# A float32 transformer block on one core: the output projection's first loads moved into attention's last head, and one small subtraction moved from VectorE to GpSimd

## The chip, the cores and the metric

One core of a Trainium2 chip. The metric is the device time of one execution in microseconds; the profile is of one such execution. TensorE is called PE, VectorE DVE, ScalarE ACT, GpSimd POOL and SyncE SP, as the profile calls them.

## The reference, cut to what matters

X has 2 sequences of 2048 tokens of 256 numbers. Four blocks follow, each added to its input: linear attention, a mixture of 16 experts (2 chosen), softmax attention, a mixture of 64 experts (8 chosen). The change is in the third:

```python
q, k, v: (2, 16 heads, 2048, 64)
scores = einsum('bhqd,bhkd->bhqk', q, k) * scale
attn = softmax(scores, axis=-1)
out = einsum('bhqk,bhkd->bhqd', attn, v)
out = out.transpose(0, 2, 1, 3).reshape(b, s, H * DH) @ w_out.T + residual
```

[...]

## The kernel before, in words

The stages run one after the other, with a barrier of all engines between them (`release`): linear attention, 16 experts, projections of q, k and v, softmax attention (`softmax_attention`), output projection with router (`output_projection`), 64 experts (`expert_pairs`).

**Softmax attention.** There are 32 heads in all (2 sequences x 16), `g` = 0 to 31, in 16 pairs (`pr`, `hh`). A head has 4 blocks of 512 queries (`qb`), a block has 8 slots, a slot `n` (0 to 31 in its head) is 512 queries against 256 keys. In a slot:

- PE makes the scores of slot n+2 (four matmuls of 512 columns, L1863 and L1864), the values of slot n (five, L1879, L1880 and L1882; six for the last slot of a block) and two matmuls of raw scores 13 slots ahead (L1847), from which only a maximum is taken. At the first slot of a block it also adds the block before's sums by a matmul, the fold (L1889).
- ACT makes `ph`, the exponential rounded to fp32r (L1815), and the same unrounded in place (L1818).
- DVE takes the low part `pl` of the exponential of slot n+1 (`low_part`, L1744) and the maximum of raw scores (`maxima`, L1724). Scores of slot n+2 wait for `pl` of slot n, because they use its PSUM.
- POOL multiplies `ph` by the low part of the first value column and adds it up (`first_sums`, L1650 to L1661: one product and one sum in each slot, none in a block's last slot). ACT's `ph` of slot n waits until the sums of slot n-4 are made; the fold waits for the last sum of its block, written to `accr`.

Once per block, in the slots with n % 8 = 2, DVE makes the stabilisers of the next block from 16 maxima (`stabilisers`, L1726 to L1737): `mg` (L1732, f32), `mh` (L1735, the same rounded to fp32r) and `ml` = `mg` - `mh` (L1737), and SP brings `mh` and `ml` as two rows into `q2` (`rows`, L1509 to L1514), for which the first scores of that block wait. In the slots 7, 9, 11 and 13 of a head DVE also cuts the raw queries and keys of the next head (`cut_low`, L1710), and POOL subtracts the cut in slots 8, 10, 12 and 14 (`take_low`, L1630). POOL splits the next head's values in the slots from 16 on (L1607, L1612, L1619), and adds two halves of a block's output in each slot with n % 8 = 5 (`whole`, L1666). The order of every engine's work is written out by hand: each engine has one stream in program order, and semaphores join them.

The excerpt that matters most, DVE's and POOL's:

```python
dve.tensor_reduce(mg[:], every, X, ALU.max).then_inc(s["mg_ready"], 1)
dve.tensor_reduce(mh[:, qb], every, X, ALU.max).then_inc(s["mg_ready"], 1)
dve.wait_ge(s["mg_ready"], 2 * (base * NQB + (qb + 1)))
dve.tensor_tensor(ml[:, qb], mg[:], mh[:, qb].bitcast(F32), ALU.subtract).then_inc(s["nm_ready"], 1)

for n in range(SLOTS):                       # POOL, head()
    first_sums(g, hh, n)
    if n % PER == 5 and g * NQB + n // PER > 0:
        whole(...)
```

**Output projection.** 8 chunks of 512 tokens. SP's queue loads, in this order: the picking matrix `sel_in` (L2009), the attention outputs and reciprocal rows of chunk 0 (`load(0)`, L1982 to L1986), the weights `wo` and `wg` (L2011, L2012), x, the softmax sums `dn` (L2014), chunk 1, x, chunk 2. ACT rounds the picking matrix (L2174) when `sel_in`, `wo` and `wg` are all there. PE waits for that and for the rows of a chunk, and spreads a reciprocal row over 128 partitions (`spread`, L2214), DVE multiplies the outputs by it (`norm`, L2058), 8 times in a chunk, and then PE multiplies with `wo` (`out_tile`, L2221). `spread(1, 0)` comes on PE right behind the first of chunk 0's four `out_tile`s.

Of the kernel before, what the change touches and what calls it, by code (L numbers as in the profile page):

```python
# [26 lines left out]
P = 128  # L27
# [6 lines left out]
QB = 512  # L34
# [106 lines left out]
class Kernel:  # L141
# [4 lines left out]
    def build(self):  # L146
# [14 lines left out]
        with ExitStack() as keep:  # L161
            self.C = keep.enter_context(nc.sbuf_tensor("C", [P, sum(w for _, w in CONST)], F32))
            self.tri = keep.enter_context(nc.sbuf_tensor("tri", [P, P], BF16))
            self.ones_bf = keep.enter_context(nc.sbuf_tensor("ones_bf", [P, P], BF16))
            self.eps = keep.enter_context(nc.sbuf_tensor("eps", [P, 2], F32))
            with ExitStack() as pw:
# [12 lines left out]
                self.raw0 = self.wup[:, 0:2].rearrange("p w n -> p (w n)").bitcast(F32R)  # L179
                self.project()  # L180
                self.release()
                self.softmax_attention()
            with ExitStack() as moe1:
                self.WR = 18
                self.sid = moe1.enter_context(nc.sbuf_tensor("sid", [P, E1 // 2], U32))
                self.sid_up = moe1.enter_context(nc.sbuf_tensor("sid_up", [CAP, E1 // 2], U32))
                self.wgu1 = moe1.enter_context(nc.sbuf_tensor("wgu1", [P, self.WR, DC, 2 * F1], F32))
                self.wd1 = moe1.enter_context(nc.sbuf_tensor("wd1", [F1 // 2, self.WR, 2, D], F32))
                self.output_projection()
                self.expert_pairs()  # L190
            self.release()
# [1217 lines left out]
    def softmax_attention(self):  # L1409
# [16 lines left out]
        with ctx:  # L1426
# [5 lines left out]
            cut = sb("cut", [P, 2, QB], U32)  # L1432
            low = sb("low", [P, 2, QB], F32R)
            vf = sb("vf", [P, 2, KC, DH])
# [23 lines left out]
            names = ("turns raw0 raw1 kq0 kq1 v0 v1 fixed cut_ready low_ready low0 low1 u_full u_max mg_ready nm_ready "  # L1458
                     "row0 row1 row2 row3 s_full p_ready pf_ready pl_ready vh_ready v_split pv_done scaled sums vl0_ready vx_ready fold_done o_added o0_low o1_low "
                     "o_ready o0_out o1_out den recip rden").split()  # L1460
# [26 lines left out]
            def _(sp):  # L1487
# [80 lines left out]
                for pr in range(1, PAIRS - 1):  # L1568
                    for hh in range(2):
# [18 lines left out]
            @block.gpsimd  # L1588
            def _(pool):
# [43 lines left out]
                def first_sums(g, hh, n):  # L1633
# [5 lines left out]
                    for j in range(2):  # L1639
# [21 lines left out]
                        pool.tensor_tensor(to, acc[:], add, ALU.add).then_inc(s["sums"], 1)  # L1661

                def whole(g, qb):

                    pool.wait_ge(s[f"o{qb % 2}_low"], 16 * ((g * NQB + qb) // 2 + 1))
                    pool.tensor_tensor(o_st[:, qb % 2], o_lo[:, qb % 2], o_all[0:DH, qb % 2], ALU.add).then_inc(s["o_added"], 1)  # L1666

                def head(pr, hh, prepare):
                    g, nxt = pr * 2 + hh, pr * 2 + (hh + 1)
                    for n in range(SLOTS):  # L1670
                        first_sums(g, hh, n)
                        if n % PER == 5 and g * NQB + n // PER > 0:
                            whole((g * NQB + n // PER - 1) // NQB, (n // PER - 1) % NQB)
# [29 lines left out]
            def _(dve):  # L1703
# [22 lines left out]
                def stabilisers(base, hh, j):  # L1726
# [71 lines left out]
            def _(act):  # L1798
# [121 lines left out]
    def output_projection(self):  # L1920
# [13 lines left out]
        with ctx:  # L1934
            wo = sb("wo", [P, G, D])
            wg = sb("wg", [P, DC, E1])
            self_in = sb("sel_in", [4 * G, G, P])
            pick = sb("pick", [4 * G, G, P], F32R)
# [4 lines left out]
            oT = sb("oT", [P, OB, G, CH])  # L1943
            rows = sb("rows", [4 * G, OB, CH], F32R)
            xs = sb("xs", [P, 2, TC, D])
# [23 lines left out]
            ps_v = ps("ps_v", [P, CH])  # L1969
            names = ("turns weights den recip low_ready rden pick_ready r_ready norm_ready o0 o1 o2 r0 r1 r2 x0 x1 out_ready added "  # L1970
                     "x0_out x1_out stat mv_ready std_ready own ln_ready xn_ready xn0_out xn1_out t_ready xT_ready l_ready "
# [7 lines left out]
            def _(sp):  # L1979
                def load(c):  # L1980
                    b, at = c * CH // L, slice(c * CH % L, c * CH % L + CH)
                    sp.dma_start(oT[:, c % OB], self.o_dram[b * G:(b + 1) * G, :, at].rearrange("g p l -> p g l"))\  # L1982
                        .then_inc(s[f"o{c % OB}"], 16)
                    for part in range(2):
                        sp.dma_start(rows[part * 2 * G:(part + 1) * 2 * G, c % OB].bitcast(F32),
                                     self.rden[part, b * 2 * G:(b + 1) * 2 * G, at]).then_inc(s[f"r{c % OB}"], 16)  # L1986
# [63 lines left out]
            def _(dve):  # L2050
                link = Chain(dve, s["own"])

                def norm(c, g):
                    if c >= NC:
                        return
                    dve.wait_ge(s[f"o{c % OB}"], 16 * (c // OB + 1))
                    dve.wait_ge(s["r_ready"], c * G + g + 1)
                    dve.tensor_tensor(oT[:, c % OB, g], oT[:, c % OB, g], ps_r[:, g % 2], ALU.mult).then_inc(s["norm_ready"], 1)  # L2058

# [104 lines left out]
            def _(act):  # L2164
# [37 lines left out]
            def _(pe):  # L2202
                pe.wait_ge(s["weights"], 48)
                pe.wait_ge(s["pick_ready"], 1)

                def spread(c, g):
# [3 lines left out]
                    if g == 0:  # L2210
                        pe.wait_ge(s[f"r{c % OB}"], 32 * (c // OB + 1))
                    if c > 0 or g > 1:
                        pe.wait_ge(s["norm_ready"], c * G + g - 1)
                    pe.matmul(ps_r[:, g % 2], pick[:, g], rows[:, c % OB], start=True, stop=True).then_inc(s["r_ready"], 1)  # L2214

                def out_tile(c, t):
# [3 lines left out]
                    for g in range(G):  # L2220
                        m = pe.matmul(ps_o[:, t % 2, 0:D], oT[:, c % OB, g, t * P:(t + 1) * P], wo[:, g],  # L2221
                                      start=g == 0, stop=g == G - 1)
# [283 lines left out]
```

## Time and profile before

| what | value |
|---|---|
| median of 3 runs | 4191.82 us (4189.85 to 4196.26) |
| the profiled execution's own time | 4191.36 us |
| its span, first to last instruction | 4189.6 us |
| mean granted TensorE clock | 0.952 |
| PE, DVE, ACT, POOL busy in the span | 90%, 81%, 63%, 73% |
| softmax attention | about 893 to 3707 us |
| output projection | from 3707 us |

A row of the timeline has the start in us from the span's start, the duration, the engine, the line, the operation with what it writes and reads, and in brackets how long the engine sat idle before it and what ended that. PE's durations overlap, since its matmuls are pipelined: one matmul's price is the time from its start to the next one's.

### The profile page before, as it was taken

The page shows a single profiled execution, that of the slowest core. Times are in us where ns is not written, and L with a number is a line of the kernel's source. Part 1 is how long each engine was busy: PE and PEld are TensorE (multiplying, and loading weights), DVE is VectorE, ACT ScalarE, POOL GpSimd, SP SyncE. Part 2 cuts the span into 40 slices and gives each one's busy share as a digit, 9 for nine tenths or more (in the row PEclk, how much of TensorE's full clock was granted, in tenths as well). Part 3 has the DMA queues.
Part 4 walks back from the last instruction along what each step waited for, and adds up shares of the span by engine and source line. Part 5 has one row for each costly group of instructions (what it writes and reads, how often), then busy time and mean ns, then how long its engine had stood idle before and what let it go on. Part 6 is the DMA issues. An engine that isn't in the chain of part 4 may idle for free. (4 is left out here: it accounts for less than half of the span.)

```text
span 4189.6 us, 55316 instructions
## 1 busy us (share of the span) xinstructions
PE 3758.9 (90%) x17018; PEld 2903.6 (69%) x17018; DVE 3392.4 (81%) x4389; ACT 2623.1 (63%) x3395; POOL 3042.9 (73%) x2832
## 2 busy tenths in 40 slices
PE   7949977869999999999999999999999999979563
PEld 4635545548888888888888888888888888857321
DVE  6845548869999999999999999999999999946511
ACT  6723333337777777777777777777777777733221
POOL 2456765758888888888888888888888888820155
PEclk9969998979999999999999999999999999989676
DMA  7123437852224332242322423224232242046295
GB/s 271 47 65 60 67 78 244 274 160 63 61 58 89 65 65 60 57 92 62 66 59 59 93 60 67 60 57 91 62 66 59 63 88 61 20 160 221 73 248 111
DMA packets 332634, 396.27 MB, mean 95 GB/s; under 512 B 142541, under 2 KB 251922, under 8 KB 319284
## 3 DMA queue, kind: packets, MB, share of 16 engines
q1 hardware_dynamic: 307702, 362.22, 33.9%
q0 software_dynamic: 24640, 30.52, 4.2%
q8 instruction: 140, 2.29, 0.2%
q14 instruction: 152, 1.24, 0.1%
HBM read 232.47 MB, written 117.79 MB: 84 GB/s over the span
## 5 line engine op out<-in xcount | busy, mean ns | idle before, releaser
L1815 ACT ACTIVATE at_ph<-at_ps_s 128x1024 fp32r<-128x1024 f32 x1024 | 1052.7, 1028 | 637.0 <-PE at_ps_s L1864 621.3
L1724 DVE TENSOR_REDUCE at_mx<-at_ps_u 128x2 f32<-128x1024 f32 x1016 | 1239.8, 1220 | 157.5 <-PE at_ps_u L1847 122.1
L1744 DVE TENSOR_TENSOR at_pl<-at_ps_s,at_ph 128x1024 fp32r<-128x1024 f32 x1024 | 1245.8, 1217 | 18.5 <-ACT at_ps_s L1818 17.4
L1818 ACT ACTIVATE at_ps_s<-at_ps_s 128x1024 f32<-128x1024 f32 x1024 | 1032.2, 1008 | 32.6
L1653 POOL TENSOR_TENSOR at_part<-at_ph,at_vl 128x512 f32<-128x512 f32 x768 | 799.0, 1040 | 114.2 <-ACT at_ph L1815 90.2
L1661 POOL TENSOR_TENSOR at_acc<-at_acc,at_part 128x512 f32<-128x512 f32 x640 | 833.5, 1302 | 50.1
L1879 PE MATMUL at_ps_v<-at_ph,at_va 128*128 128x512 f32 x2048 | 812.2, 397 | 1.1 <-DVE at_pl L1744 1.1
L1880 PE MATMUL at_ps_v<-at_pl,at_va 128*128 128x512 f32 x2048 | 812.9, 397 | 0.0
L1882 PE MATMUL at_ps_v<-at_ph,at_vx 128*128 128x512 f32 x1152 | 456.2, 396 | 0.0
L1880 PEld LDWEIGHTS at_ps_v<-at_pl,at_va 128*128 128x128 f32 x2048 | 387.4, 189 | 90.4
L1863 PE MATMUL at_ps_s<-q,k 128*128 128x512 f32 x1024 | 410.9, 401 | 21.6 <-DVE at_pl L1744 19.5
L1863 PE MATMUL at_ps_s<-at_q,at_k 128*128 128x512 f32 x1024 | 411.0, 401 | 20.5 <-DVE at_pl L1744 20.2
L1879 PEld LDWEIGHTS at_ps_v<-at_ph,at_va 128*128 128x128 f32 x2048 | 388.0, 189 | 46.8 <-DVE at_pl L1744 1.7
L1864 PE MATMUL at_ps_s<-at_q,k 66*128 66x512 f32 x1024 | 407.2, 398 | 0.0
L1864 PE MATMUL at_ps_s<-at_q,at_k 66*128 66x512 f32 x1024 | 406.9, 397 | 0.0
L1847 PE MATMUL at_ps_u<-k,q 128*128 128x512 f32 x1008 | 327.3, 406 | 36.6 <-DMA at_q<-at_low 31.3
L1847 PE MATMUL at_ps_u<-at_k,at_q 128*128 128x512 f32 x1024 | 328.7, 402 | 3.8 <-DVE at_mx L1724 3.8
L1847 PEld LDWEIGHTS at_ps_u<-k,q 128*128 128x128 f32 x1008 | 275.0, 311 | 70.2 <-issue 31.7
L1847 PEld LDWEIGHTS at_ps_u<-at_k,at_q 128*128 128x128 f32 x1024 | 279.6, 310 | 34.9 <-DVE at_mx L1724 13.6
L1863 PEld LDWEIGHTS at_ps_s<-q,k 128*128 128x128 f32 x1024 | 193.8, 189 | 89.6 <-DVE at_pl L1744 44.3
L1863 PEld LDWEIGHTS at_ps_s<-at_q,at_k 128*128 128x128 f32 x1024 | 193.4, 189 | 90.0 <-DVE at_pl L1744 47.5
L1882 PEld LDWEIGHTS at_ps_v<-at_ph,at_vx 128*128 128x128 f32 x1152 | 216.2, 188 | 52.6
(285 smaller groups left out, 5446.3 us busy)
## 6 DMA issues: line engine op xcount, KB each, us to landing
wgu<-Wgu_in SPq DMA_DIRECT2D x64, 384.0 KB, 5.1
qT<-pj_rot SPq DMA_DIRECT2D x32, 512.0 KB, 5.2
vT<-pj_vo SPq DMA_DIRECT2D x16, 1024.0 KB, 5.7
kT<-pj_rot SPq DMA_DIRECT2D x32, 512.0 KB, 3.2
k<-kT SPq DMA_DIRECT2D x32, 512.0 KB, 11.6
q<-qT SPq DMA_DIRECT2D x32, 512.0 KB, 9.5
at_q<-at_low SPq DMA_DIRECT2D x128, 128.0 KB, 2.3
at_vf<-vT SPq DMA_DIRECT2D x32, 512.0 KB, 8.7
```

The lines of the kernel that those rows point to most:

```text
L1653: pool.tensor_tensor(add, p, low0, ALU.mult).then_inc(s["scaled"], 1)
L1661: pool.tensor_tensor(to, acc[:], add, ALU.add).then_inc(s["sums"], 1)
L1724: dve.tensor_reduce(mx[:, qb % 2, 2 * i:2 * i + 2], maxima_at(base, j)[:, 0:2], X, ALU.max).then_inc(s["u_max"], 1)
L1744: dve.tensor_tensor(pl[:, n % NP], ps_s[:, n % 2], ph[:, n % NP].bitcast(F32), ALU.subtract)\
L1815: act.activation(ph[:, n % NP], ps_s[:, n % 2], ACT.Exp, scale=DH ** -0.5)\
L1818: act.activation(ps_s[:, n % 2], ps_s[:, n % 2], ACT.Exp, scale=DH ** -0.5)\
L1847: m = pe.matmul(maxima_at(base, j)[:, w], tile, k1[hh][:, kb * QB:(kb + 1) * QB], start=True, stop=True)
L1863: pe.matmul(out, k1[hh][:, ks], q1[hh][:, qs], start=True, stop=False)
L1864: m = pe.matmul(out, k2[hh][0:MROW + 2, ks], q2[hh][0:MROW + 2, qs], start=False, stop=True)
L1879: pe.matmul(out, va[:, hh, c], ph[:, n % NP, keys], start=c == 0, stop=False)
L1880: m = pe.matmul(out, va[:, hh, c], pl[:, n % NP, keys], start=False, stop=False)
L1882: m = pe.matmul(out, vx[:, hh, own_product(c)], ph[:, n % NP, keys], start=False, stop=False)
```

## The change

`ml` is computed by POOL. Its new function `low_stabilisers(block_)` waits for DVE's `mg` and `mh` and stands, in each slot with n % 8 = 2, between `first_sums` and whatever POOL does next; DVE's own wait and subtraction are gone.

```diff
@@ gpsimd
+                def low_stabilisers(block_):
+                    pool.wait_ge(s["mg_ready"], 2 * (block_ + 1))
+                    pool.tensor_tensor(ml[:, block_ % NQB], mg[:], mh[:, block_ % NQB].bitcast(F32), ALU.subtract)\
+                        .then_inc(s["nm_ready"], 1)
@@ head(), gpsimd
                         first_sums(g, hh, n)
+                        if n % PER == 2 and g * NQB + n // PER + 1 < HEADS * NQB:
+                            low_stabilisers(g * NQB + n // PER + 1)
                         if n % PER == 5 and g * NQB + n // PER > 0:
@@ before the heads, gpsimd
+                low_stabilisers(0)
@@ stabilisers(), vector
-                    dve.wait_ge(s["mg_ready"], 2 * (base * NQB + (qb + 1)))
-                    dve.tensor_tensor(ml[:, qb], mg[:], mh[:, qb].bitcast(F32), ALU.subtract).then_inc(s["nm_ready"], 1)
```

The loads of the projection's chunk 0 and of the picking matrix are issued by SP ahead of attention's last head, into buffers of their own (the matrix goes through `raw[0]`, which is free by then), and ACT rounds the matrix at the end of attention. To make room, `low` moves onto a weight buffer that is free in attention.

```diff
@@ build()
+                self.oT0 = early("oT0", [P, H // 2, QB], F32)
+                self.rows0 = early("rows0", [2 * H, QB], F32R)
+                self.pick = early("pick", [2 * H, H // 2, P], F32R)
                 self.softmax_attention()
@@ softmax_attention()
-            low = sb("low", [P, 2, QB], F32R)
+            low = self.wup[:, 2].rearrange("p (i n) -> p i n", i=2).bitcast(F32R)
@@ sync, softmax_attention()
                 head(PAIRS - 1, 0, False, False)
+                sp.wait_ge(s["rden"], 32)
+                sp.dma_start(self.oT0[:], self.o_dram[0:H // 2, :, 0:QB].rearrange("g p l -> p g l")).then_inc(s["next_in"], 16)
+                for part in range(2):
+                    sp.dma_start(self.rows0[part * H:(part + 1) * H].bitcast(F32), self.rden[part, 0:H, 0:QB]).then_inc(s["next_in"], 16)
+                sp.dma_start(raw[0][0:2 * H, 0:H // 2 * P].bitcast(F32), self.ins["sel"]).then_inc(s["pick_in"], 16)
                 head(PAIRS - 1, 1, False, True)
...
-                sp.wait_ge(s["rden"], 32)
+                sp.wait_ge(s["next_in"], 48)
@@ scalar, softmax_attention(), at the end
                 output(HEADS - 1, NQB - 1)
+                act.wait_ge(s["pick_in"], 16)
+                act.activation(self.pick[:], raw[0][0:2 * H, 0:H // 2 * P].bitcast(F32).rearrange("k (g m) -> k g m", g=H // 2),
+                               ACT.Copy).then_inc(s["pick_out"], 1)
@@ sync, output_projection()
-                sp.dma_start(self_in[:], ins["sel"].rearrange("k (g m) -> k g m", g=G)).then_inc(s["weights"], 16)
-                load(0)
@@ scalar, output_projection()
-                act.wait_ge(s["weights"], 48)
-                act.activation(pick[:], self_in[:], ACT.Copy).then_inc(s["pick_ready"], 1)
@@ tensor, output_projection()
-                pe.wait_ge(s["weights"], 48)
-                pe.wait_ge(s["pick_ready"], 1)
...
                 for g in range(G):
                     spread(0, g)
+                pe.wait_ge(s["weights"], 32)
                 for c in range(NC + 2):
```

In the projection `oT` and `rows` are now three tensors each instead of one tensor with three parts, the first of them being `oT0` and `rows0`, and the waits of chunk 0 on their loads fall away.

## Rows read from the trace of the kernel before

**Rows 1.** Windows: busy time of each engine, clock, DMA, in attention and at the projection's start

```profile
core 0: us, PE busy (x) PEld busy (x) DVE busy (x) ACT busy (x) POOL busy (x), PEclk, DMA share, GB/s
915.00:3697.00 2782.00, 2734.51 (x11479) 2255.54 (x11479) 2605.89 (x2543) 2145.99 (x2173) 2376.36 (x2255) 1.00 0.31 65
...
3710.00:3725.00 15.00, 2.92 (x5) 1.34 (x5) 2.37 (x4) 2.34 (x2) 0.00 (x0) 0.50 1.07 366
```

**Rows 2.** Groups by line, 915 to 3697 us: DVE's subtraction and cut, POOL's smallest subtraction

```profile
L1737 DVE TENSOR_TENSOR at_ml<-at_mg,at_mh 128x4 fp32r<-128x4 f32 x127 | 88.1, 694 | 4.4
L1710 DVE TENSOR_SCALAR at_cut<-at_raw 128x512 uint32<-128x512 uint32 x64 | 46.6, 729 | 0.0
...
L1619 POOL TENSOR_TENSOR at_vl<-at_vf,at_va 128x16 f32<-128x16 f32 x31 | 7.6, 246 | 0.0
```

**Rows 3.** Timeline of DVE in head 12 and the next: mh, ml, cut

```profile
1970.42 0.16 DVE L1735 TENSOR_REDUCE at_mh<-at_mx 128x4 fp32r<-128x16 f32 x1
1970.61 1.06 DVE L1737 TENSOR_TENSOR at_ml<-at_mg,at_mh 128x4 fp32r<-128x4 f32 x1
...
1988.03 1.47 DVE L1710 TENSOR_SCALAR at_cut<-at_raw 128x512 uint32<-128x512 uint32 x1
...
1993.02 0.16 DVE L1735 TENSOR_REDUCE at_mh<-at_mx 128x4 fp32r<-128x16 f32 x1
1993.21 0.16 DVE L1737 TENSOR_TENSOR at_ml<-at_mg,at_mh 128x4 fp32r<-128x4 f32 x1
...
2014.41 0.48 DVE L1737 TENSOR_TENSOR at_ml<-at_mg,at_mh 128x4 fp32r<-128x4 f32 x1
...
2080.09 0.16 DVE L1735 TENSOR_REDUCE at_mh<-at_mx 128x4 fp32r<-128x16 f32 x1
```

**Rows 4.** Timeline of PE in head 12: the stalls and the two folds

```profile
1971.90 0.40 PE L1882 MATMUL at_ps_v<-at_ph,at_vx 128*128 128x512 f32 x1
1972.86 0.50 PE L1863 MATMUL at_ps_s<-q,k 128*128 128x512 f32 x1 [0.56 <-DVE at_pl L1744]
1973.20 0.39 PE L1864 MATMUL at_ps_s<-at_q,k 66*128 66x512 f32 x1
...
1990.69 0.86 PE L1847 MATMUL at_ps_u<-k,q 128*128 128x512 f32 x2 [0.28 <-DVE at_mx L1724]
...
2006.80 0.40 PE L1889 MATMUL at_ps_v<-at_accr,at_first 128*128 128x512 f32 x1
...
2028.15 0.39 PE L1889 MATMUL at_ps_v<-at_accr,at_first 128*128 128x512 f32 x1
...
2038.00 0.50 PE L1863 MATMUL at_ps_s<-q,k 128*128 128x512 f32 x1 [0.55 <-DVE at_pl L1744]
```

**Rows 5.** Timeline of POOL in head 12

```profile
1970.36 1.29 POOL L1661 TENSOR_TENSOR at_acc<-at_acc,at_part 128x512 f32<-128x512 f32 x1
...
1987.93 1.30 POOL L1661 TENSOR_TENSOR at_acc<-at_acc,at_part 128x512 f32<-128x512 f32 x1
1989.58 1.28 POOL L1630 TENSOR_TENSOR at_low<-at_raw,at_cut 128x512 fp32r<-128x512 f32 x1 [0.36 <-DVE at_cut L1710]
...
2002.16 1.29 POOL L1661 TENSOR_TENSOR at_accr<-at_acc,at_part 128x512 fp32r<-128x512 f32 x1
...
2022.97 1.29 POOL L1661 TENSOR_TENSOR at_accr<-at_acc,at_part 128x512 fp32r<-128x512 f32 x1
```

**Rows 6.** Timeline, from attention's end to the first output tile

```profile
3707.26 0.34 SPq L2009 DMA_DIRECT2D op_sel_in<-sel_in  x1
...
3720.25 1.05 ACT L2174 ACTIVATE op_pick<-op_sel_in 32x1024 fp32r<-32x1024 f32 x1 [19.86 <-DMA op_wg<-router_in]
3721.41 1.19 PE L2214 MATMUL op_ps_r<-op_rows,op_pick 32*128 32x512 f32 x2 [21.65 <-ACT op_pick L2174]
...
3728.53 5.24 PE L2221 MATMUL op_ps_o<-op_wo,op_oT 128*128 128x256 f32 x16 [0.85 <-DVE op_oT L2058]
```

**Rows 7.** DMA issues, 3697 to 3900 us: KB each, median us to landing

```profile
op_oT<-o_dram SPq DMA_DIRECT2D x8, 2048.0 KB, 9.3
...
op_wo<-w_outT_in SPq DMA_DIRECT2D x1, 1024.0 KB, 9.9
op_rows<-rden SPq DMA_DIRECT2D x16, 32.0 KB, 8.2
```

More of the change, by code:

```diff
@@ L165, in build @@
             self.eps = keep.enter_context(nc.sbuf_tensor("eps", [P, 2], F32))
+            moe1 = keep.enter_context(ExitStack())
             with ExitStack() as pw:
@@ L181, in build @@
                 self.release()
+                early = lambda name, shape, dt: moe1.enter_context(nc.sbuf_tensor(name, shape, dt))
+                self.oT0 = early("oT0", [P, H // 2, QB], F32)
+                self.rows0 = early("rows0", [2 * H, QB], F32R)
+                self.pick = early("pick", [2 * H, H // 2, P], F32R)
                 self.softmax_attention()
[L183 to L190, printed above, removed]
+            self.WR = 18
+            self.sid = moe1.enter_context(nc.sbuf_tensor("sid", [P, E1 // 2], U32))
+            self.sid_up = moe1.enter_context(nc.sbuf_tensor("sid_up", [CAP, E1 // 2], U32))
+            self.wgu1 = moe1.enter_context(nc.sbuf_tensor("wgu1", [P, self.WR, DC, 2 * F1], F32))
+            self.wd1 = moe1.enter_context(nc.sbuf_tensor("wd1", [F1 // 2, self.WR, 2, D], F32))
+            self.output_projection()
+            self.expert_pairs()
             self.release()
@@ L1458, in softmax_attention @@
             names = ("turns raw0 raw1 kq0 kq1 v0 v1 fixed cut_ready low_ready low0 low1 u_full u_max mg_ready nm_ready "
-                     "row0 row1 row2 row3 s_full p_ready pf_ready pl_ready vh_ready v_split pv_done scaled sums vl0_ready vx_ready fold_done o_added o0_low o1_low "
+                     "row0 row1 row2 row3 s_full p_ready pf_ready pl_ready vh_ready v_split pv_done scaled sums vl0_ready vx_ready fold_done o_added o0_low o1_low next_in pick_in pick_out "
                      "o_ready o0_out o1_out den recip rden").split()
@@ L1936, in output_projection @@
             wg = sb("wg", [P, DC, E1])
-            self_in = sb("sel_in", [4 * G, G, P])
-            pick = sb("pick", [4 * G, G, P], F32R)
+            pick = self.pick
             dn = sb("dn", [P, H * L // P])
@@ L1942, in output_projection @@
             rl = sb("rl", [P, H * L // P], F32R)
-            oT = sb("oT", [P, OB, G, CH])
-            rows = sb("rows", [4 * G, OB, CH], F32R)
+            oT = [self.oT0] + [sb(f"oT{i}", [P, G, CH]) for i in range(1, OB)]
+            rows = [self.rows0] + [sb(f"rows{i}", [4 * G, CH], F32R) for i in range(1, OB)]
             xs = sb("xs", [P, 2, TC, D])
@@ L1969, in output_projection @@
             ps_v = ps("ps_v", [P, CH])
-            names = ("turns weights den recip low_ready rden pick_ready r_ready norm_ready o0 o1 o2 r0 r1 r2 x0 x1 out_ready added "
+            names = ("turns weights den recip low_ready rden r_ready norm_ready o0 o1 o2 r0 r1 r2 x0 x1 out_ready added "
                      "x0_out x1_out stat mv_ready std_ready own ln_ready xn_ready xn0_out xn1_out t_ready xT_ready l_ready "
@@ L1981, in load @@
                     b, at = c * CH // L, slice(c * CH % L, c * CH % L + CH)
-                    sp.dma_start(oT[:, c % OB], self.o_dram[b * G:(b + 1) * G, :, at].rearrange("g p l -> p g l"))\
+                    sp.dma_start(oT[c % OB][:], self.o_dram[b * G:(b + 1) * G, :, at].rearrange("g p l -> p g l"))\
                         .then_inc(s[f"o{c % OB}"], 16)
                     for part in range(2):
-                        sp.dma_start(rows[part * 2 * G:(part + 1) * 2 * G, c % OB].bitcast(F32),
+                        sp.dma_start(rows[c % OB][part * 2 * G:(part + 1) * 2 * G].bitcast(F32),
                                      self.rden[part, b * 2 * G:(b + 1) * 2 * G, at]).then_inc(s[f"r{c % OB}"], 16)
@@ L2055, in norm @@
                         return
-                    dve.wait_ge(s[f"o{c % OB}"], 16 * (c // OB + 1))
+                    if c > 0:
+                        dve.wait_ge(s[f"o{c % OB}"], 16 * (c // OB + (c % OB > 0)))
                     dve.wait_ge(s["r_ready"], c * G + g + 1)
-                    dve.tensor_tensor(oT[:, c % OB, g], oT[:, c % OB, g], ps_r[:, g % 2], ALU.mult).then_inc(s["norm_ready"], 1)
+                    dve.tensor_tensor(oT[c % OB][:, g], oT[c % OB][:, g], ps_r[:, g % 2], ALU.mult).then_inc(s["norm_ready"], 1)
                 def add(c, t):
@@ L2210, in spread @@
                     if g == 0:
-                        pe.wait_ge(s[f"r{c % OB}"], 32 * (c // OB + 1))
+                        if c > 0:
+                            pe.wait_ge(s[f"r{c % OB}"], 32 * (c // OB + (c % OB > 0)))
                     if c > 0 or g > 1:
                         pe.wait_ge(s["norm_ready"], c * G + g - 1)
-                    pe.matmul(ps_r[:, g % 2], pick[:, g], rows[:, c % OB], start=True, stop=True).then_inc(s["r_ready"], 1)
+                    pe.matmul(ps_r[:, g % 2], pick[:, g], rows[c % OB][:], start=True, stop=True).then_inc(s["r_ready"], 1)
                 def out_tile(c, t):
@@ L2220, in out_tile @@
                     for g in range(G):
-                        m = pe.matmul(ps_o[:, t % 2, 0:D], oT[:, c % OB, g, t * P:(t + 1) * P], wo[:, g],
+                        m = pe.matmul(ps_o[:, t % 2, 0:D], oT[c % OB][:, g, t * P:(t + 1) * P], wo[:, g],
                                       start=g == 0, stop=g == G - 1)
```

## The prediction, before the change was run

> **What bounds the kernel now.** First the windows by stage: from 915 to 3697 us, two thirds of the span, PE is busy 2734.51 of 2782.00 us at full granted clock, POOL 2376.36, DVE 2605.89 [rows 1]. So attention is PE's, and a gain there has to be a stall of PE that the change removes. The pattern repeats with each head; one period, from `mh` at 1993.02 to the same `mh` of the next head at 2080.09, is 87.07 us [rows 3].
>
> Second the groups by line: `ml`, four numbers per partition, takes DVE 694 ns on average, 88.1 us in all, and the cut 729 ns [rows 2]. The timeline says why these are not short: in one block `ml` takes 0.16 us, in others 0.48 and 1.06 [rows 3]. The one of 1970.61 ends at 1971.67, when POOL's sum of 1970.36 ends at 1971.65 [rows 5]. A DVE instruction that reads two SBUF tiles waits out the GpSimd instruction that is running. The cut of 1988.03 behaves alike: 1.47 us, until 1989.50, with POOL's sum of 1987.93 ending at 1989.23 [rows 3, 5].
>
> Third PE's timeline, where that is paid. PE normally starts a matmul 0.23 us after the last. Here 1971.90 is followed by 1972.86, then 1973.20: 0.73 and 0.11 us lost, 0.84, waiting for `pl`, which stood behind the long `ml`. The stall at 2038.00 (0.55 us idle against 0.56) is its twin in the last block, 0.82. Both vanish without `ml`. The block with `ml` of 0.48 should lose about 0.26 (the 0.84 less the 0.58 by which `ml` is shorter). The fourth loss, about 0.9 around 1990.69, waits for a maximum that stood behind the long cut [rows 3, 4]; there `ml` took 0.16 only and is not the cause. Together about 2.8 us of a head's 87.07.
>
> Fourth the projection. Its first load is issued at 3707.26, PE's first matmul starts at 3721.41 and the first output tile at 3728.53 [rows 6]: 21.27 us in which DMA is the work (share 1.07, 366 GB/s) at half clock [rows 1].
>
> **The projection's part.** Call 3707.26 T0; barrier and SP's order before it stay. The picking matrix, chunk 0 and ACT's rounding (1.05 us [rows 6]) leave the path. PE can spread at about T0 instead of T0+14.15, and the eight spreads and norms take the 7.12 us from 3721.41 to 3728.53: T0+7.1. The weights (1088 KB) are now first in the queue. By the rate of rows 1 they take 3.0 us and some start; from above, `wo` landed after 9.9 us with 2 MB ahead of it [rows 7], so T0+5 to T0+10.4; I take T0+7, hidden behind the norms. The first tile costs 5.24 us as before [rows 6], the clock being at the same half. So 14.2 us are gained up to T0+12.3. Next late is chunk 1: its spread is right behind the first tile, and ahead of its rows 1024+64+512+128+2048 KB, 3.87 MB, go through at 366 GB/s, 10.6 us, plus about 3.7 of start and landing (an estimate; the landing alone is up to 8.2 [rows 7]): T0+14.3. PE waits 2 us. Sum: -12 us, between -9 and -14. Later chunks keep their order and their work, only earlier.
>
> The moved loads are issued around 3610 us, ahead of the last head: 2048 KB land in 9.3 us [rows 7] while DMA is a third busy [rows 1], and the first thing behind them on SP, the low rows of the last head's predecessor, is due only when that head has run two slots. I cost them and ACT's copy at nothing. If that cover is gone, one late row is some 5 us once. The same for moving `low`, and for splitting `oT` and `rows`: other addresses, same work.
>
> **Attention's part, DVE's side.** Removed: 128 waits and subtractions, `mh` is now followed by `pl` at once. That takes 0.84+0.82+0.26 us of PE's stalls away: 85.15 us a head if nothing else is late. At once 31 heads x 1.9 = 60 us.
>
> **Attention's part, GpSimd's side.** Added: 128 subtractions of 128x4. The nearest row is the 128x16 one, 246 ns [rows 2]; I take 0.25. From below, 0.16 as on DVE [rows 3]; from above, 1.30 as the big sums [rows 5], should such an instruction's price lie in its start.
>
> But the wait matters more. In the second block POOL has finished its slot at 1989.23 (1987.93+1.30) and goes on with `take_low` at 1989.58, while `mh` is ready at 1993.18 (1993.02+0.16) [rows 3, 5]. POOL will stand 3.9 us with `take_low` and everything after it queued behind. In the first block it stands 4.3 us too, but has idle time to make that good. From 1989.58 on it has none: it runs without a pause (its timeline has no idle entry) up to the last sum of the third block, which ends at 2024.26: 34.68 us. The folds wait for these sums. Today they have 3.35 us to spare in one block (2002.16+1.29 against 2006.80) and 3.89 in the next (2024.26 against 2028.15) [rows 4, 5]. POOL comes later by 1993.18+0.07+0.25-1989.58 = 3.9 us, and by 4.2 after the second small subtraction, while PE comes earlier. So the folds become late, and the pace is set by a loop through POOL:
>
> - fold at 2028.15 to `mh` ready in the next head, 2080.25: 52.10 today, less the stalls 0.82 and 0.84 in it: 50.4. The cut before this `mh` will meet a product of 1.04 instead of a sum of 1.30; I take 0.2 off: 50.2.
> - `mh` to the last sum of the third block: 0.1 + 0.25 + 34.68 + 0.25 = 35.3.
> - sum to fold: 0.1.
>
> 85.6 us against 87.07: 1.47 x 31 heads = 46 us, of which the loop takes back only 0.45 a head from the 85.15 above. The last head prepares none and adds nothing that I count. The row of `ml` comes to SP later, by the 0.3 us of the subtraction, or by POOL's lag in the third block; it is needed four slots (10 us) on and its transfer is small: hidden.
>
> **Sum against the profiled execution's 4191.36 us:** -12 -46 = 4133, median of the runs 0.5 us above that; I say 4134.
>
> A rule of the Trainium skill speaks against this half. "Perfetto Trace Analysis", section "Optimizing Scalar/DVE Operations", says that GpSimd and VectorE share an SBUF port, so that moving work between the two may not help. The trace shows the shared waiting (0.16 against 1.06 us). By the rule attention would stay, and the sum would be that of the third case below.
>
> **The rivals.** 0.2%, 8.4 us, is about what can be told from no change.
>
> 1. *GpSimd's wait paces attention at about 85.6 us a head* (85.1 to 86.3): 4110 to 4155, point 4134. For: the folds' small spare time and POOL without a pause. Chance 0.52.
> 2. *The cut falls free.* The cut's start and POOL's product before it are within 0.3 us in my walk; if POOL is a little later, the cut costs 0.42 instead of 1.47, `mh` comes 1.05 earlier, the loop is 84.6 and PE's own pace 85.15-0.88 = 84.3. Some 2.5 to 2.8 x 31 = 78 to 87 us: 4092 to 4101. Against: more often GpSimd is running than not (2376 of 2782 us). Chance 0.2.
> 3. *The port's wait comes back at the cuts.* The change would then not do what it says: four cuts a head, 0.729 us on average today, up to 1.47. With POOL shifted by 4 us, three more long ones are 3 us, in the slots where DVE has no slack, and eat up what `ml` gave. Only the projection's 12 remain: 4179, from 4165 to 4190. Against: two of the four come where `take_low` now starts later. Chance 0.18.
> 4. *Slower.* The stretch of GpSimd between `mh` and the last sum of the third block decides from 87.07-50.4-0.1 = 36.6 us; above 37.0 it also eats the projection's 12 us. With a small subtraction at 1.30 us instead of 0.25 it is 34.68+2.6+0.1 = 37.4, the loop 87.9, +0.85 x 31 = +26 -12: 4206. For: GpSimd is given work just where it is fullest. Against: 128x16 costs 246 ns, 31 times. Chance 0.1.
>
> **How the numbers follow.** The forecast is case 1. The range 4088 to 4178 holds cases 1 and 2 and half of case 3, 0.8. Faster by over 0.2% (under 4183): cases 1, 2 and two thirds of 3, 0.83. Within 0.2%: the rest of 3 and some of 4, 0.10. Slower: 0.07.
>
> **What would show it.** In the timeline after: no stall of PE behind `pl` in the first and last block of a head; POOL idle some 4 us before its new subtraction in the first two blocks, none in the third; PE waiting for `accr` before the fold in the second or third block, 0.2 to 1 us; the `mh` to `mh` period about 85.6. The first output tile 7 us after the projection's first load instead of 21.27, and a short wait before `spread(1, 0)`. I am wrong if the small subtraction takes near 1 us, if the cuts' mean moves much from 729 ns, if ACT rather than the fold waits for POOL, or if the first tile waits for weights past T0+10.

## The result, and the profile after

**Slower.** The changed kernel takes 4275.83 us, median of 4 runs (4267.39 to 4284.77), beside 4191.28 us for the kernel before in the same series (4 runs). The ratio is 1.020, with a 95% interval from 1.018 to 1.022: clearly slower, by about 2%. The profiled execution spans 4265.6 us, 76 more than before.

| | before | after |
|---|---|---|
| median of the runs, us | 4191.28 | 4275.83 |
| span of the profile, us | 4189.6 | 4265.6 |
| mean granted clock | 0.952 | 0.943 |
| SP issues the projection's first load at | 3707.26 | 3798.56 |
| from there to the first expert's memset | 247.06 | 233.48 |
| from the memset to the end | 235.3 | 233.6 |
| mean head (from one slot 0's exponential to the next, heads 1 to 30) | 87.10 | 90.29 |

The projection gained 13.6 us and the experts 1.7. Attention lost 91.3, counted up to the projection's first load. First the projection, where the timeline after answers to [rows 6]:

```profile
3798.56 0.42 SPq L2025 DMA_DIRECT2D op_wo<-w_outT_in  x1
...
3798.61 1.19 PE L2225 MATMUL op_ps_r<-rows,pick 32*128 32x512 f32 x2 [7.51 <-PEq L1430]
...
3805.55 6.73 PE L2232 MATMUL op_ps_o<-op_wo,oT 128*128 128x256 f32 x16 [0.87 <-DVE oT L2073]
...
3812.92 0.50 PE L2225 MATMUL op_ps_r<-op_rows,pick 32*128 32x512 f32 x1 [0.65 <-DMA op_rows<-rden]
```

PE spreads at once, and the first tile starts 6.99 us after the first load instead of 21.27. Now attention; first two groups by line from 915 to 3785 us:

```profile
L1727 DVE TENSOR_SCALAR at_cut<-at_raw 128x512 uint32<-128x512 uint32 x64 | 41.5, 649 | 0.0
L1674 POOL TENSOR_TENSOR at_ml<-at_mg,at_mh 128x4 fp32r<-128x4 f32 x127 | 25.5, 201 | 266.0 <-DVE at_mh L1752 266.0
```

The moved subtraction is short, 201 ns where `ml` took 694 on DVE, and the cut of `raw` takes 649 ns instead of 729 [rows 2]. But POOL stands 266 us in front of it. The windows, in the form of [rows 1], show a PE that is busy for less of the time, and a clock that is not full:

```profile
core 0: us, PE busy (x) PEld busy (x) DVE busy (x) ACT busy (x) POOL busy (x), PEclk, DMA share, GB/s
2005.00:2012.00 7.00, 3.36 (x15) 2.57 (x14) 4.75 (x4) 3.04 (x3) 4.97 (x6) 1.00 0.63 127
2013.00:2016.00 3.00, 3.00 (x8) 2.31 (x7) 1.39 (x2) 1.99 (x2) 2.32 (x2) 0.50 0.19 44
915.00:3785.00 2870.00, 2762.78 (x11469) 2292.48 (x11468) 2524.43 (x2414) 2142.47 (x2169) 2384.87 (x2377) 0.98 0.30 64
```

In 915 to 3785 us PE is idle 107 us of 2870, before 47 of 2782. What it waits for is in the waits of that stretch (engine, line, what it waited for: us in total, times, longest):

```profile
POOL at_ml L1674 <- DVE at_mh L1752: 266.0, 96, 6.2
...
PE at_ps_s L1880 <- DMA at_q<-at_ml: 97.7, 31, 3.9
ACT at_ph L1829 <- POOL at_accr L1670: 62.7, 53, 1.5
...
PE at_ps_v L1906 <- POOL at_accr L1670: 5.2, 28, 0.2
```

PE waits for the DMA that carries a row of `ml` into `q`: in each of heads 1 to 30 for 2.5 to 3.9 us at the first scores of the second block, and now and then for a moment elsewhere. PE's waits before have no such line. The 97.7 us are more than attention lost; the timeline of PE after shows one case:

```profile
2007.70 0.40 PE L1899 MATMUL at_ps_v<-at_ph,at_vx 128*128 128x512 f32 x1
2011.74 0.48 PE L1880 MATMUL at_ps_s<-q,k 128*128 128x512 f32 x1 [3.64 <-DMA at_q<-at_ml]
...
2013.09 0.63 PE L1897 MATMUL at_ps_v<-at_pl,at_va 128*128 128x512 f32 x1
...
2014.37 0.63 PE L1896 MATMUL at_ps_v<-at_ph,at_va 128*128 128x512 f32 x1
2014.80 0.63 PE L1897 MATMUL at_ps_v<-at_pl,at_va 128*128 128x512 f32 x1
2015.22 0.63 PE L1899 MATMUL at_ps_v<-at_ph,at_vx 128*128 128x512 f32 x1
```

PE stands 3.64 us. Soon behind the stall the matmuls start 0.43 us apart instead of 0.23: the window 2013 to 2016 has a granted clock of 0.50, the lower of the two levels (1.2 GHz), where the stretch before the stall had 1.00. This does not follow every stall. Of heads 1 to 30, 16 have a stretch of some 3 us at the lower clock, 7 have one of nearly 7 us, and 7 (heads 1, 2, 9 and 26 to 29, with stalls of 2.9 to 3.4 us) have none. The trace thus gives the price by itself: less its own stall, a head takes 85.8 us without the fall, 86.8 with the short one and 88.2 with the long one. On average that is another 1.1 us a head; by the matmuls' spacing it is 1.4.

**Why is the row late?** SP issues it no later in the head than before. Head 12 of the kernel before begins (its first exponential) at 1957.37, the same head after at 1988.05. SP's timeline of the kernel before, rows that were not shown above (SPq is SP's queue; the second column is how long SP issues):

```profile
1953.68 0.47 SPq L1526 DMA_DIRECT2D o_dram<-at_o_st  x1
...
1955.06 0.51 SPq L1489 DMA_DIRECT2D at_raw<-qT  x1
...
1956.97 4.79 SPq L1496 DMA_DIRECT2D at_k<-kT  x1
...
1972.35 0.59 SPq L1514 DMA_DIRECT2D at_q<-at_ml  x1
```

and the same instructions after:

```profile
1989.30 0.47 SPq L1530 DMA_DIRECT2D o_dram<-at_o_st  x1
...
1990.69 0.51 SPq L1493 DMA_DIRECT2D at_raw<-qT  x1
...
1992.59 4.81 SPq L1500 DMA_DIRECT2D at_k<-kT  x1
...
2002.23 0.59 SPq L1518 DMA_DIRECT2D at_q<-at_ml  x1
```

From the head's start the row of `ml` is issued at +14.98 us before and at +14.18 after. The store of the head's third output block moved from -3.69 to +1.25: 4.9 us later. SP issues in order, and behind that store stand the 3.5 MB of loads for later heads: `raw` and `v` (1.5 MB) for the head after next, `q` and `k` (2 MB) for the next. They moved along, and the small rows are now issued while these are still in flight. The row took this long from issue to landing (all 128 rows, of four blocks in each head; first before, then after):

```profile
DMA to landing us min/median/max: 1.9/2.0/4.6
```

```profile
DMA to landing us min/median/max: 1.9/2.0/9.7
```

The long ones are those of the second block: 3.5 us on average before, 9.0 after (heads 1 to 30), where the other blocks' rows keep 2.0 to 2.2. In head 12 the row is issued at 2002.23, PE would take it at 2007.93 (0.23 us after its last matmul), 5.7 us later, and it lands after 9.4 us, at 2011.60. In windows of the trace after, the DMA share is about 1.0 to 1.2 from 1992 to 2007 us, 0.82 from 2007 to 2010 and 0.02 from 2010 to 2012: the row lands when the loads are through.

And why is the store late? It waits for `whole` of slot 29, a sum of POOL. The timelines before and after, rows of POOL and, for `mh` of slot 26 (the last block's), of DVE:

```profile
1948.51 0.16 DVE L1735 TENSOR_REDUCE at_mh<-at_mx 128x4 fp32r<-128x16 f32 x1
...
1952.29 1.29 POOL L1666 TENSOR_TENSOR at_o_st<-at_o_lo,at_o_all 64x512 f32<-64x512 f32 x1
```

```profile
1980.05 0.16 DVE L1752 TENSOR_REDUCE at_mh<-at_mx 128x4 fp32r<-128x16 f32 x1
...
1980.29 0.20 POOL L1674 TENSOR_TENSOR at_ml<-at_mg,at_mh 128x4 fp32r<-128x4 f32 x1 [0.50 <-DVE at_mh L1752]
...
1987.91 1.29 POOL L1680 TENSOR_TENSOR at_o_st<-at_o_lo,at_o_all 64x512 f32<-64x512 f32 x1
...
2001.35 0.20 POOL L1674 TENSOR_TENSOR at_ml<-at_mg,at_mh 128x4 fp32r<-128x4 f32 x1 [3.46 <-DVE at_mh L1752]
...
2027.82 0.20 POOL L1674 TENSOR_TENSOR at_ml<-at_mg,at_mh 128x4 fp32r<-128x4 f32 x1 [4.23 <-DVE at_mh L1752]
```

Before, POOL had gone past slot 26 by the time `mh` was ready: `whole` starts 3.62 us after it (1952.29 less 1948.67). Now POOL's slot 26 cannot begin its subtraction before `mh`, and three slots of sums of 2.56 us stand between it and `whole`, which starts 7.70 us after `mh` (1987.91 less 1980.21).

So the theory to test is a chain through three in-order queues: POOL waits for `mh`, `whole` of slot 29 ends late, SP's store and the 3.5 MB behind it go out late, the row of the second block lands late, PE stalls, and the clock falls behind the stall. Rivals: the long stay of POOL itself paces PE (the loop through POOL, which the prediction's first case rests on, mis-sized); or the fallen clock comes from the new mix of work and not from the stall; or the projection's moved loads are to blame.

### The profile page after: what moved, and what is told of

It reads as the page before. It is cut to its first block and busy times, and to the rows that moved or that the text cites. A ratio compares the mean times of both kernels' runs of the same rounds, so it can differ in the third digit from the quotient of the medians.

```text
span 4265.6 us, 55308 instructions
## 1 busy us (share of the span) xinstructions
PE 3787.4 (89%) x17018; PEld 2942.5 (69%) x17018; DVE 3313.5 (78%) x4261; ACT 2622.2 (61%) x3395; POOL 3056.2 (72%) x2960
## 5 line engine op out<-in xcount | busy, mean ns | idle before, releaser
L1896 PE MATMUL at_ps_v<-at_ph,at_va 128*128 128x512 f32 x2048 | 822.0, 401 | 1.0 <-DVE at_pl L1758 1.0
L1897 PE MATMUL at_ps_v<-at_pl,at_va 128*128 128x512 f32 x2048 | 822.7, 402 | 0.0
L1897 PEld LDWEIGHTS at_ps_v<-at_pl,at_va 128*128 128x128 f32 x2048 | 393.5, 192 | 91.3
```

The costliest lines, as they stand in the source:

```text
L1896: pe.matmul(out, va[:, hh, c], ph[:, n % NP, keys], start=c == 0, stop=False)
L1897: m = pe.matmul(out, va[:, hh, c], pl[:, n % NP, keys], start=False, stop=False)
```

## The experiments

Times are medians, or the one run where there is one; the kernel before stood at 4185.4 to 4191.3 in the series. "Head" is the mean distance of the starts of heads 1 to 31, 87.10 us for the kernel before.

### One half alone: `prefetch_only` and `subtract_only`

`prefetch_only` keeps the projection's part and gives the subtraction back to DVE. `subtract_only` keeps attention's part.

```diff
 # prefetch_only
                     dve.tensor_reduce(mh[:, qb], every, X, ALU.max).then_inc(s["mg_ready"], 1)
+                    dve.wait_ge(s["mg_ready"], 2 * (base * NQB + (qb + 1)))
+                    dve.tensor_tensor(ml[:, qb], mg[:], mh[:, qb].bitcast(F32), ALU.subtract).then_inc(s["nm_ready"], 1)
...
-                        if n % PER == 2 and g * NQB + n // PER + 1 < HEADS * NQB:
-                            low_stabilisers(g * NQB + n // PER + 1)
```

> The change's projection part alone; the subtraction stays on VectorE. All theories: attention stays at 87.1 us a head, the first output tile starts 7 us after the projection's first load instead of 21.3, and the total falls by 13 to 14 us, to about 4178 us. If moving tiles to other addresses or the moved loads had slowed attention, heads would be longer than 87.1 us here.

Measured: 4177.24 us (7 runs) against 4191.03, ratio 0.997 (0.9959 to 0.9982); head 87.06. The first tile starts 6.96 us after SP's first load.

```diff
 # subtract_only
-                sp.dma_start(self.oT0[:], self.o_dram[0:H // 2, :, 0:QB].rearrange("g p l -> p g l")).then_inc(s["next_in"], 16)
...
+                sp.dma_start(self_in[:], ins["sel"].rearrange("k (g m) -> k g m", g=G)).then_inc(s["weights"], 16)
```

> The change's attention part alone. Theory L (late loads: GpSimd's wait in slot 10 makes the half sum 'whole' of slot 29 late, so SyncE issues 3.5 MB of loads late, and the stabiliser rows queue behind them): heads of 90.3 us, a stall of PE of 3.7 us in slot 6 of each head that ends with the DMA of ml, total 4191 + 98 = about 4289 us. If the slow down came from the early loads, the moved tile 'low' or the splitting of oT, this kernel stays below 4191 us.

Measured: 4279.31 us in one run, some 10 us under what was expected; head 90.29, clock 0.942. Its wait for the row:

```profile
PE at_ps_s L1868 <- DMA at_q<-at_ml: 100.7, 32, 4.6
```

The projection's part is a gain of about 14 us, and is cleared. The whole loss is in the subtraction's move.

### Is the DVE gain real: `no_low`

The kernel before, with no subtraction at all: POOL clears `ml` once, and the rows are released by `mh`. It leaves out the low part of the stabilisers.

```diff
-                    dve.tensor_reduce(mh[:, qb], every, X, ALU.max).then_inc(s["mg_ready"], 1)
-                    dve.wait_ge(s["mg_ready"], 2 * (base * NQB + (qb + 1)))
-                    dve.tensor_tensor(ml[:, qb], mg[:], mh[:, qb].bitcast(F32), ALU.subtract).then_inc(s["nm_ready"], 1)
+                    dve.tensor_reduce(mh[:, qb], every, X, ALU.max).then_inc(s["nm_ready"], 1)
```

> No low part of the stabilisers is computed at all: a row of zeros stands in its place, and the rows are released by mh. It prices VectorE's side alone. If the prediction's count of stalls is right: heads of 85.15 us, total 4191 - 60 = 4131 us, with cuts still at 0.7 us on average. If the port's wait comes back at the cuts: heads of 86.5 us or more, 4175 us or more.

Measured: 4128.38 us, head 85.17, with the old projection. The prediction's count of the stalls behind `ml` gave 85.15. The one stall left in a head, 0.6 us, is the one behind the long cut, which stays at 740 ns:

```profile
L1714 DVE TENSOR_SCALAR at_cut<-at_raw 128x512 uint32<-128x512 uint32 x64 | 47.4, 740 | 0.0
```

### The late store alone: `whole_late`

The kernel before, with `whole` one slot later in the last block. No subtraction moves and POOL waits for no `mh`.

```diff
-                        if n % PER == 5 and g * NQB + n // PER > 0:
+                        if n % PER == (6 if n // PER == 3 else 5) and g * NQB + n // PER > 0:
```

> The kernel before, in which only the half sum 'whole' of a head's third block is made one slot later (slot 30 instead of 29), so that SyncE's store, and the 3.5 MB of loads behind it, come 3.5 us later. The stabilisers are as before. Theory L: some 2 us of that are spare, the rest shows as a stall of PE before the first scores of the next head's second block that ends with the DMA of the ml row; with the clock's fall 1.5 to 2.6 us a head, total 4235 to 4270 us. Theory P (only the folds or ACT waiting for GpSimd's sums cost anything) and theory N (the row is late because ml is computed late): within 10 us of 4191 us.

Measured: 4224.96 us, head 88.34, clock 0.952 as before. The row lands after up to 7.4 us, and PE waits for it in 30 heads, which it never did before:

```profile
PE at_ps_s L1863 <- DMA at_q<-at_ml: 28.8, 30, 1.7
```

One line of POOL's order, without any of the change, makes the kernel 34 us slower by the same wait. So the late store alone is enough for a stall of this kind, without any wait of POOL for `mh`; whether POOL's waiting costs something besides, this run does not tell, but the next ones do. It came out under what was expected: `whole` ended at -0.36 us from the head's start (before -3.71, after +1.13), so it is a smaller dose, and behind stalls of 1.2 us on average the clock fell in one head of heads 1 to 30 only, the one with the longest (1.8 us; granted clock 0.50 from 3051 to 3054 us).

### The chain cut on SP: `loads_first` and `store_behind`

Both are the changed kernel, with POOL's order as it is. `loads_first` issues `raw` and `v` (1.5 MB) of the head after next ahead of the late store, and the other 2 MB stay behind it; `store_behind` issues that store behind all 3.5 MB.

```diff
 # loads_first
-                def head(pr, hh, first, last):
+                def head(pr, hh, first, last, next_loads=None):
...
                             rows(*after, 0)
+                        if qb == NQB - 1 and next_loads is not None:
+                            ahead(*next_loads)
                         if block_ > 0:
                             store_o((block_ - 1) // (2 * NQB), (block_ - 1) // NQB % 2, (block_ - 1) % NQB)
...
-                    head(0, hh, True, False)
-                    ahead(0, hh)
+                    head(0, hh, True, False, (0, hh))
```

```diff
 # store_behind
                         load_qk(*after)
+                    if (2 * pr + hh) > 0:
+                        store_o((2 * pr + hh - 1) // 2, (2 * pr + hh - 1) % 2, NQB - 2)
...
-                        if block_ > 0:
+                        if block_ > 0 and (qb < NQB - 1 or last):
```

> The changed kernel, in which SyncE issues the 1.5 MB of raw and value loads ahead of the head's last store instead of behind it, so that only 2 MB stand behind the late half sum. GpSimd's wait is as in the changed kernel. Theory L: the stall of PE in slot 6 (3.7 us) and the fall of the clock behind it vanish, heads of 85.5 to 86.3 us (the loop through the folds of the prediction is then what is left), total 4130 to 4155 us. If GpSimd's lateness costs through anything else (folds, ACT, ml made late), heads stay near 90.3 us and the total near 4270 us.

> The changed kernel, in which the head's last store (of the half sum that is late) is issued behind the 3.5 MB of loads, so that none of them waits for GpSimd. Theory L: as the run loads_first or slightly faster, total 4125 to 4155 us, and PE never waits for the DMA of ml. A theory in which it is the amount of traffic and not its place behind the half sum: no better than the changed kernel.

Measured: `loads_first` 4124.82 us (4 runs), ratio 0.984 (0.982 to 0.986), head 85.34, clock 0.952, the slowest landing 3.7 us. `store_behind` 4120.97 us, head 85.33, slowest landing 3.4 us. Both are some 5 us faster than the ranges on record. The waits for `mh` and for POOL's sums in `loads_first`:

```profile
POOL at_ml L1674 <- DVE at_mh L1752: 218.0, 96, 4.9
...
ACT at_ph L1829 <- POOL at_accr L1670: 63.4, 54, 1.5
```

`loads_first` is the run that decides. POOL stands 218 us for `mh` here too and ends `whole` as late as in the changed kernel (+1.13 us), yet attention takes 85.34 us a head. POOL's waiting costs PE almost nothing by itself. With the stall the falls of the clock in heads 1 to 30 are gone as well, while the work is the same: they belong to the stall and not to the new mix.

### The chain cut on POOL: `slot3` and `slot4`

The changed kernel, with the subtraction one or two slots later in each block.

```diff
-                        if n % PER == 2 and g * NQB + n // PER + 1 < HEADS * NQB:
+                        if n % PER == 4 and g * NQB + n // PER + 1 < HEADS * NQB:    # slot3: 3
```

> The changed kernel with the subtraction on GpSimd one slot later in its program (slots with n % 8 = 3 instead of 2), SyncE's order as in the changed kernel. In the kernel before, the sums of slot 11 ended at the moment at which mh of that block was ready, so the 3.9 us wait there falls to under 0.5 us while the subtraction itself stays on GpSimd. Theory L: half sum of slot 29 on time, no stall in slot 6, folds on time, heads of 85.1 to 85.4 us, total 4115 to 4125 us. If the instruction on GpSimd costs, not its wait: no better than 4200 us.

> As slot3, but in the slots with n % 8 = 4: no wait for mh at all on GpSimd, but the row of ml goes out some 2.5 us later. It has about 3 us less than the four slots that it had. Expected 4115 to 4130 us; if the row is late in the third or fourth block, a stall that ends with the DMA of ml shows there and the total is above that of slot3.

Measured: `slot3` 4142.72 us (4 runs), ratio 0.989 (0.988 to 0.991), head 86.03; `slot4` 4118.20 us, head 85.28. The waits of `slot3`:

```profile
POOL at_ml L1674 <- DVE at_mh L1752: 89.2, 96, 2.4
...
PE at_ps_s L1880 <- DMA at_q<-at_ml: 21.4, 28, 1.2
```

`slot3` was a miss, some 20 us over what was expected. I had taken the chain to have a slack that one slot would restore; `whole` still ends at -1.42 us, 2.3 us later than before, and 0.96 us a head of the stall is left. In `slot4` POOL waits for no `mh` but the first, `whole` ends at -2.48, and PE's waits for the row come to 1.1 us in all.

### Which of POOL's waits: `wait_26_only` and `wait_10_only`

The subtraction in slot 4 of each block, but for one block where it stays in slot 2: the last one (slot 26), or the second (slot 10).

```diff
-                        if n % PER == 2 and g * NQB + n // PER + 1 < HEADS * NQB:
+                        if n % PER == (2 if n // PER == 3 else 4) and g * NQB + n // PER + 1 < HEADS * NQB:    # wait_10_only: == 1
```

> The changed kernel with GpSimd's subtraction in slots 4, 12, 20 of a head (no wait for mh there) but still in slot 26 for the last block, where GpSimd has finished its sums about 4 us before mh is ready. If the late half sum of slot 29 comes from this last wait, three slots of sums before it: the half sum ends about 9 us behind mh of slot 26, against 5 us in the kernel before, 2 us more than is spare: a stall of PE of 1.5 to 2.5 us in slot 6 that ends with the DMA of ml, total 4165 to 4200 us. If only the lag collected since slot 10 matters, as in the prediction's walk: no stall, total 4115 to 4125 us.

> The reverse: the subtraction in slot 10 with its wait of about 4 us, in slots 4, 20 and 28 for the other blocks. If the lag since slot 10 is enough by itself, the half sum of slot 29 comes some 4 us late and the stall is there as well, 1 to 2.5 us, total 4150 to 4200 us; folds and ACT wait too, as in loads_first. If the wait in slot 26 is the whole cause: as loads_first, 4120 to 4130 us.

Measured: `wait_26_only` 4257.38 us, head 90.01; `wait_10_only` 4236.87 us, head 88.96. Both are misses: I expected each to carry a part of the loss, and the first carries all of it. The waits, first of `wait_26_only`, then of `wait_10_only`:

```profile
POOL at_ml L1674 <- DVE at_mh L1752: 115.8, 31, 5.2
...
PE at_ps_s L1880 <- DMA at_q<-at_ml: 98.3, 30, 3.9
```

```profile
PE at_ps_s L1880 <- DMA at_q<-at_ml: 76.3, 51, 2.4
```

The waits of POOL don't add. With slot 26 alone POOL stands 3.7 us there (115.8 over 31), where after the changed kernel's earlier waits it stands 0.6 on average (0.50 in the row of 1980.29 us); either way three slots of sums follow `mh` before `whole`, which ends at +1.13 in both. In `wait_10_only` the wait in slot 8's scores is only about 0.57 us, and a new one of 2.2 to 2.5 us a head appears at slot 24: that row's subtraction now stands in slot 20 of a POOL that slot 10 has put behind. The row there lands 2.0 us after its issue, so it is issued late and not held up on the way. That is a lag and a late place together, which this run does not separate; that slot 20 alone is harmless `slot4` shows.

### Both cures: `slot4_loads_first`

The edits of `slot4` and `loads_first` together.

> Both cures together: the subtraction in slots with n % 8 = 4 and the 1.5 MB of loads ahead of the last store. Each alone left under 0.3 us a head that the other can take away. Expected heads of 85.0 to 85.1 us, total 4112 to 4118 us, the fastest of all so far.

Measured: 4111.14 us (5 runs, 4110.37 to 4115.64) against 4185.39, ratio 0.982 (0.980 to 0.984); head 85.09, clock 0.952. PE waits for no row of `ml` any more. It is the fastest kernel here, 1.8% under the one before.

**All of them on one scale.** Where `whole` of slot 29 ends, counted from the next head's start (mean of heads 2 to 30), where the row of that head's second block lands on the same count, and the stall in front of slot 8's scores (heads 1 to 30):

| kernel | `whole` ends at, us | row lands at, us | stall, us a head | slowest landing, us | head, us |
|---|---|---|---|---|---|
| before | -3.71 | +18.45 | 0 | 4.6 | 87.10 |
| `slot4` | -2.48 | +19.69 | 0.15 | 5.2 | 85.28 |
| `wait_10_only` | -2.00 | +20.12 | 0.57 | 6.2 | 88.96 (stall in slot 24) |
| `slot3` | -1.42 | +20.65 | 0.96 | 6.9 | 86.03 |
| `whole_late` | -0.36 | +21.73 | 1.21 | 7.4 | 88.34 |
| `wait_26_only` | +1.13 | +23.21 | 4.05 | 8.1 | 90.01 |
| after | +1.13 | +23.18 | 3.86 | 9.7 | 90.29 |
| `loads_first` | +1.13 | +16.35 | 0 | 3.7 | 85.34 |

The row lands later by nearly as much as `whole` ends later (1.2, 1.7, 2.2, 3.3, 4.8 and 4.7 us, against 1.2, 1.7, 2.3, 3.4, 4.8 and 4.8). Its own issue hardly matters: `wait_26_only` issues it 1.6 us later in the head than the changed kernel and it lands at the same point. With the same late `whole`, but 1.5 of the 3.5 MB issued ahead of it, it lands in time and there is no stall. The stall is the distance from slot 7's exponential to slot 8's, less the usual 2.57 us; for `wait_26_only` and the changed kernel it includes scores made at the lower clock, and PE's own gap is 3.4 us.

## Why the prediction was wrong

**The step that failed** is the last sentence of attention's GpSimd side: "The row of `ml` comes to SP later [...]; it is needed four slots (10 us) on and its transfer is small: hidden." The row did come in time to SP (0.8 us earlier in the head than before). Its transfer is small, but in the second block's traffic it took 9.0 us on average and up to 9.7, and not 2.0. The spare time was mis-sized too: between the row's issue and PE's need lie 5.7 us and not 10, and before the change that row already took 3.5 us of them. What was not asked is what else POOL's wait holds back. I followed the queue behind the waiting instruction through POOL's sums to the folds; `whole` is in the same queue, and the store that waits for it stands in SP's queue ahead of 3.5 MB, which stand ahead of the row. Some 1 us of delay was nearly free (`slot4`, 0.15 us of stall), the change made 4.8.

**The wait in the last block** was left out: I named waits in the first two blocks and said the first had idle time to make them good. By `wait_26_only` the one in the last block is enough for the loss.

**Point by point.**

- Projection, -12 (-9 to -14): right, -13.6. First tile predicted 7.1 us after T0, measured 6.99; `spread(1, 0)` predicted at T0+14.3 after a 2 us wait, measured at T0+14.36 (3812.92 less 3798.56), with 0.65 us idle named. The first tile took 6.73 us, not the 5.24 I had kept; chunk 1 set the time, so it cost nothing. That chunk 1 came within 0.1 us of its forecast is partly luck, since 3.7 us of it were an estimate. The loads moved into attention cost nothing, as `prefetch_only` shows.
- The stalls behind `ml`, 0.84 + 0.82 + 0.26: right. `no_low` gave 85.17 us a head against 85.15.
- The subtraction at 0.25 us: 0.20. POOL's wait of 3.9 us in the second block: 4.2; of 4.3 in the first: 3.5. The folds do wait for POOL, 0.2 us each, and ACT does, 1.2 us at a time (62.7 over 53), which the text had named as a sign of error; `loads_first` has both, so together they cost PE about 0.4 us a head at most.
- The loop, 85.6 us a head: `loads_first`, where the late row is gone and POOL's wait is left, has 85.34, and the fold at the third block's start waits for POOL in nearly every head, as the prediction had it. Against 85.09 in `slot4_loads_first` this costs 0.25 us a head, where the prediction had 0.45. So the mechanism of the first case was there, smaller than forecast, and a second one lay over it.
- Attention as a whole: forecast -46 us, measured +91. A head: the stall of 3.4 us (PE's own gap) and the lower clock's 1.1 to 1.4 add 4.5 to 4.8, the waits for POOL's sums 0.4; the vanished stalls take off 1.9 and a shorter one behind the cut 0.4. That is 2.6 to 2.9 of the 3.2 us measured (90.29 less 87.10). Heads 0 and 31 have no such stall, so this holds for 30 of the 32.
- The slower case was given 0.1 in all, by a long small subtraction. That did not happen. Its sign was right by another mechanism.
- The port's wait: by the rule cited from the Trainium skill ("Perfetto Trace Analysis", "Optimizing Scalar/DVE Operations") moving work between VectorE and GpSimd might not help. The prediction made of it a case in which the cuts grow longer, and that did not come. Leaving DVE's port wait behind is worth 1.9 us a head here, and `slot4` keeps 1.8 of it with the subtraction on GpSimd; the cuts of `raw` did not grow longer in the changed kernel (649 ns, before 729).

**What stays open.** Why the clock fell behind 23 stalls of heads 1 to 30 and not behind the other 7, which are of the same length, is not shown. The row lands when the loads are through and not a fixed time after its issue, which speaks for its standing behind them, but no run issues it on another queue. What slot 10's lag alone costs in `wait_10_only` is not separated. The 4 runs of the changed kernel spread over 17 us, more than those of any cure; the two slower ones have the lower mean clocks (0.939 and 0.938, the others 0.943 and 0.942).

## What to carry to other kernels

Before a wait is put into an in-order queue, list every instruction behind it whose result another in-order queue waits for, and do the same again for that queue: a big load that starts late delays a small one that starts on time. A transfer's median landing time holds only for the traffic it was measured in; when loads move in time, look at what small transfers they now cover. When an operation goes to another engine, put it where its input is already there: two slots later was worth 158 us here (4118.20 us against 4275.83).

## What the runs showed of the hardware

- A row of 4 numbers per partition lands 2.0 us after its issue in the median and up to 9.7 us when it is issued behind 3.5 MB of loads that started late; with these loads issued ahead of the late store the slowest is 3.4 (`store_behind`).
- Behind stalls of 2.7 to 4.1 us, one in each of heads 1 to 30, the granted clock fell from 1.00 to 0.50 in 23 of the 30 (matmuls 0.43 us apart from 2013.09 to 2016.08) and stayed at 1.00 in 7; in `wait_26_only`, with stalls of 2.6 to 4.1 us, it fell in all 30. It fell 7 times in `wait_10_only`, behind stalls of 2.3 to 2.5 us, and once in `whole_late`, behind 1.8 us; the mean clock (0.951 and 0.952) hardly shows it.
- A subtraction of 128x4 takes 201 ns on GpSimd, less than a third of the 694 ns that it took on DVE, where it waited for GpSimd's sums (0.16 us where it met none, 1.06 behind a sum).
